# An audio tower with a shared and a routed feed-forward part on one core: the shared down product in three rounded products instead of one full-precision product

## The reference

```python
h = (ewma(x) + ewma_reversed(x)) * 0.5 @ W.T + b            # tokens: 16 x 750 rows of 256
h = h + selective_scan_two_layers(layernorm(h))             # 64 states
n = layernorm(h)
shared = (silu(n @ shared_gate_w.T) * (n @ shared_up_w.T)) @ shared_down_w.T   # 512 hidden
topk_idx, w = route(n)          # 16 experts in 4 groups, 2 groups and 4 experts of each token
routed = sum over the chosen experts e of w_e * (silu(n @ gate_w[e]) * (n @ up_w[e])) @ down_w[e]
out = h + shared + routed
```

## Time and profile before

| what | us |
|---|---|
| median of three runs (1314.46 to 1319.79) | 1316.31 |
| the profiled execution's own time | 1317.08 |
| its span, first to last instruction | 1314.9 |
| granted TensorE clock, mean | 0.943 of full speed |

### The profile page before, as it was taken

One profiled execution on the slowest core, in us unless ns is written; L12 is line 12 of the kernel. 1 busy time (PEld: TensorE's weight loads), 2 busy tenths in 40 slices (PEclk: granted clock), 3 DMA queues, 4 the chain that ended last, 5 costly groups with the idle time before them and its releaser, 6 DMA issues.

```text
span 1314.9 us, 24750 instructions
## 1 busy us (share of the span) xinstructions
PE 1167.5 (89%) x7477; PEld 1051.9 (80%) x7477; DVE 942.2 (72%) x2374; ACT 552.3 (42%) x899; POOL 415.4 (32%) x281
## 2 busy tenths in 40 slices
PE   3448877987999889998999899997999999989997
PEld 3337766866998789977988789977998899889997
DVE  6786898698668975888668975798578855644443
ACT  1524542552355333653355244553465343223332
POOL 2023162043212623153412623163302430343233
PEclk9658885998999989999999999999999999999999
DMA  4130021132021312231131323240221321243331
GB/s 124 32 88 24 17 69 36 44 84 56 12 55 33 99 50 53 42 83 45 31 70 31 79 54 53 42 98 26 42 62 34 91 38 38 55 104 56 53 50 20
DMA packets 88288, 71.48 MB, mean 54 GB/s; under 512 B 39671, under 2 KB 82848, under 8 KB 88168
## 3 DMA queue, kind: packets, MB, share of 16 engines
q1 hardware_dynamic: 58832, 43.30, 12.1%
q0 software_dynamic: 26832, 26.06, 11.9%
q10 hardware_dynamic: 2504, 0.55, 0.2%
HBM read 31.36 MB, written 39.34 MB: 54 GB/s over the span
## 4 chain that ended last, share of the span: by engine, by line
PE 66%; DVE 24%; issue 7%; ACT 1%; POOL 1%; DMA 0%; DVEq 0%; POOLq 0%; ACTq 0%
PE gu_ps L1692 18%; PE gu_ps L1665 14%; PE d_ps L1752 10%; PE d_ps L1733 8%; PE ch_ps L1642 3%; PE ch_ps L1720 3%; DVE h L1188 2%; DVE h L1196 2%; PE ch_ps L1573 2%; DVE stats L1202 1%; PE ch_ps L1712 1%; DVE h L1464 1%; DVE gu_ps L1453 1%; PE ch_ps L1603 1%; PE ch_ps L1591 1%
## 5 line engine op out<-in xcount | busy, mean ns | idle before, releaser
L804 POOL DMA_INDIRECT out_dram<-block_rows,entry x99 | 158.1, 1597 | 319.1 <-ACT block_rows L944 298.4
L1692 PE MATMUL gu_ps<-gu_hi,bx_hi 128*128 x792 | 238.7, 301 | 17.6 <-issue 17.6
L1692 PE MATMUL gu_ps<-gu_hi,bx_lo 128*128 x792 | 225.4, 285 | 0.0
L1692 PE MATMUL gu_ps<-gu_lo,bx_hi 128*128 x792 | 225.4, 285 | 0.0
L932 ACT ACTIVATE hid<-gu_ps 128x512 f32<-128x512 f32 (+1 forms) x195 | 115.1, 592 | 241.9 <-PE gu_ps L1692 108.7
L785 POOL DMA_INDIRECT lists<-records,pos x96 | 136.1, 1418 | 203.8 <-DVE pos L1361 177.9
L1733 PE MATMUL d_ps<-down,hid 128*125 128x256 f32 x768 | 185.3, 385 | 1.2 <-issue 1.2
L1692 PEld LDWEIGHTS gu_ps<-gu_hi,bx_hi 128*128 128x128 f32 x792 | 152.4, 192 | 26.1 <-issue 24.8
L1733 PEld LDWEIGHTS d_ps<-down,hid 128*125 128x125 f32 x768 | 140.7, 190 | 20.8 <-issue 1.8
L1692 PEld LDWEIGHTS gu_ps<-gu_hi,bx_lo 128*128 128x128 f32 x792 | 152.6, 193 | 1.2
L1692 PEld LDWEIGHTS gu_ps<-gu_lo,bx_hi 128*128 128x128 f32 x792 | 151.6, 191 | 0.0
(11 more groups left out here) (279 smaller groups left out, 2893.3 us busy)
## 6 DMA issues: line engine op xcount, KB each, us to landing
block_rows<-lists SPq DMA_DIRECT2D x99, 128.0 KB
out_dram<-h SPq DMA_DIRECT2D x24, 500.0 KB
t<-rstd_scratch SPq DMA_DIRECT2D x21, 250.0 KB, 5.2
x_in<-in_x_dram SPq DMA_DIRECT2D x8, 375.0 KB, 7.6
zt<-in_x_dram SPq DMA_DIRECT2D x7, 375.0 KB
entry<-lists SPq DMA_DIRECT2D x99, 8.0 KB, 2.5
out_dram<-block_rows,entry POOLq DMA_INDIRECT x99
lists<-records,pos POOLq DMA_INDIRECT x96
```

The lines of the kernel that those rows point to most:

```text
L804: pool.indirect_dma_start(out=out_rows[0:there, :], out_offset=bass.IndirectOffsetOnAxis(entry[n % UE][:, ID:ID + 1].bitcast(U32), 0), in_ ...
L1692: last = pe.matmul(gu_ps[:, 2 * (g % 2) + half, q * GH:(q + 1) * GH], a[n % 2][:, k, :], w[:, k, bass.ds(of, 1), half * GH:(half + 1) * GH ...
```

## The change

The down weights of the shared part are kept as a rounded part and a rest, both of type fp32r, and each fp32 matmul of `shared_down` becomes three fp32r matmuls. The parts of the hidden units are made by ScalarE (rounded, a copy) and GpSimd (rest, a subtraction), into the two buffers each that blocks use. `shared_down` waits for the rest (`s_lo`) instead of the hidden units. `hid`, the gathered rows and the finished blocks have rings of three instead of four. The group registers of up to two coming blocks are loaded behind a shared down product. Due ticks of some steps change, above all those of the list writes on GpSimd. `s_count(pair, n)` counts shared slots.

```diff
-    ("list", 0, dict(POOL=12.5)),
+    ("list", 0, dict(POOL=15.0)),
...
+    ("list", 1, dict(POOL=15.0)),
+    ("list", 2, dict(POOL=15.0)),
...
+    ("list", 3, dict(POOL=15.5)),
+    ("list", 4, dict(POOL=16.5)),
+    ("list", 5, dict(POOL=17.0)),
+    ("list", 7, dict(POOL=17.0)),
+    ("list", 6, dict(POOL=17.5)),
...
-    U, UE, UO = 4, 12, 4
+    U, UE, UO = 3, 12, 3
...
-        down = sb("down", [P, M, D])
+        down_hi, down_lo = (sb(f"down_{s}", [P, M, D], F32R) for s in ("hi", "lo"))
...
-        hid_t = sb("hid", [P, 4, 512])
+        NH = 3
+        hid_t = sb("hid", [P, NH, 512])
...
+            def shared_lo(pair, n, g):
+                wait(pool, "s_hi", s_count(pair, n))
+                inc(pool.tensor_tensor(hid_lo[g % 2][:, 0:TT], hid[g % NH][:, 0:TT],
+                                       hid_hi[g % 2][:, 0:TT].bitcast(F32), ALU.subtract), "s_lo")
+
             for k, before, g, amid in ticks("POOL"):
+                if g is not None and slot(g - 2)[0] == "S":
+                    shared_lo(*slot(g - 2)[1:], g - 2)
                 for event in before + amid:
...
-                was = slot(g - 4)
+                was = slot(g - NH)
                 if was[0] == "S":
-                    wait(act, "down_mm", done(g - 4))
+                    wait(act, "s_lo", s_count(*was[1:]))
...
+            def shared_hi(pair, n, g):
+                wait(act, "hid_done", done(g))
+                wait(act, "down_mm", done(g - 2))
+                inc(act.activation(hid_hi[g % 2][:, 0:TT], hid[g % NH][:, 0:TT], ACT.Copy), "s_hi")
...
                 run(amid)
                 if slot(g - 2)[0] == "B":
                     block_hi(slot(g - 2)[1], g - 2)
+                elif slot(g - 2)[0] == "S":
+                    shared_hi(*slot(g - 2)[1:], g - 2)
...
+            def groups_ahead(g):
+
+                ahead = []
+                for k in range(g + 1, g + 8):
+                    if slot(k)[0] == "S":
+                        break
+                    if slot(k)[0] == "B" and slot(k)[1] not in group_of:
+                        ahead.append(slot(k)[1])
+                for n in ahead[:2]:
+                    load_groups(n)
...
             def shared_down(pair, n, g):
                 m = n % M
-                wait(pe, "hid_done", done(g))
+                wait(pe, "s_lo", s_count(pair, n))
...
-                    last = pe.matmul(d_ps[0:TP, j, :], hid[g % 4][:, tc], down[:, m, :],
-                                     start=(m == 0 and j % 2 == 0), stop=(m == M - 1), skip_group_check=True)
+                    for c, (a, w) in enumerate(((hid_hi, down_hi), (hid_hi, down_lo), (hid_lo, down_hi))):
+                        last = pe.matmul(d_ps[0:TP, j, :], a[g % 2][:, tc], w[:, m, :],
+                                         start=(m == 0 and j % 2 == 0 and c == 0), stop=(m == M - 1 and c == 2),
+                                         skip_group_check=True)
                 inc(last, "down_mm")
...
                     shared_down(*slot(g - 3)[1:], g - 3)
+                    groups_ahead(g)
```

More of the change, by code:

```diff
@@ L133 @@
     (1, "table", 0): dict(DVE=14.5),
-    (0, "list", 0): dict(POOL=11.0),
+    (0, "list", 0): dict(POOL=15.0),
     (0, "ln1_stats", 0): dict(POOL=-26.5),
-    (0, "list", 8): dict(POOL=12.5),
+    (0, "list", 8): dict(POOL=15.0),
     (1, "ln2_norm", 1): dict(ACT=-1.5),
@@ L157 @@
     (0, "list", 11): dict(POOL=19.0),
[L158 to L161, removed]
+    (1, "list", 1): dict(POOL=15.0),
+    (1, "list", 2): dict(POOL=15.0),
+    (1, "list", 3): dict(POOL=15.0),
+    (1, "list", 4): dict(POOL=15.0),
     (1, "list", 5): dict(POOL=16.0),
@@ L174 @@
     (0, "spread", 0): dict(SP=-19.5),
-    (1, "list", 0): dict(POOL=11.5),
+    (1, "list", 0): dict(POOL=15.0),
     (1, "spread", 0): dict(SP=-26.0),
@@ L192 @@
     (1, "residual", 5): dict(DVE=-1.5),
+    (2, "list", 0): dict(POOL=15.5),
+    (0, "table", 0): dict(DVE=15.0),
+    (1, "entries", 0): dict(DVE=14.0),
+    (0, "list", 1): dict(POOL=16.0),
+    (0, "x2t", (0, 1)): dict(ACT=-3.0),
+    (0, "x2t", (1, 0)): dict(ACT=-0.5),
+    (0, "x2t", (1, 1)): dict(ACT=1.0),
+    (0, "ln2_norm", 2): dict(ACT=1.5),
+    (0, "x2t", (2, 0)): dict(ACT=3.0),
 }
@@ L216 @@
     (8.4, "routed", 4),
-    (11.4, "routed", 5),
+    (9.4, "routed", 5),
     (-6.7, "shared", 5),
@@ L365, in audio_tower_kernel @@
         states = sb("states", [P, 2, T], F32R)
-        hid_t = sb("hid", [P, 4, 512])
-        hid = [hid_t[:, n, :] for n in range(4)]
+        NH = 3
+        hid_t = sb("hid", [P, NH, 512])
+        hid = [hid_t[:, n, :] for n in range(NH)]
         hid_hi = [sb(f"hid_hi{n}", [P, 512], F32R) for n in range(2)]
@@ L583, in shared_part @@
                 return [w[:, n % KD, :].rearrange("p (m c) -> p m c", m=M) for w in pair_]
-            return down[:, :, (n % KD) * P:(n % KD + 1) * P], None
+            return [w[:, :, (n % KD) * P:(n % KD + 1) * P] for w in (down_hi, down_lo)]
         def shared_view(n):
@@ L931, in silu @@
                 hidden_is_free(g)
-                inc(act.activation(hid[g % 4][:, 0:n], gu_ps[:, 2 * (g % 2), 0:n], ACT.Silu), "silu_done")
+                inc(act.activation(hid[g % NH][:, 0:n], gu_ps[:, 2 * (g % 2), 0:n], ACT.Silu), "silu_done")
             def block_x(n, g):
@@ L1440, in shared_hidden @@
             def shared_hidden(g):
-                h = hid[g % 4][:, 0:TT]
+                h = hid[g % NH][:, 0:TT]
                 wait(dve, "prod_mm", done(g))
@@ L1454, in block_hidden @@
                 else:
-                    h = hid[g % 4].rearrange("p (e h) -> p e h", h=H)
+                    h = hid[g % NH].rearrange("p (e h) -> p e h", h=H)
                     wait(dve, "up_weighed", n + 1)
@@ L1698, in _, with load_groups @@
             group_of = {}
+            def load_groups(n):
+                if n in group_of:
+                    return
+                if n == first[iteration[n]]:
+                    wait(pe, "tabled", iteration[n])
+                group_of[n] = [pe.value_load(table[0:1, 3 * n + 1 + q:3 * n + 2 + q], min_val=0, max_val=NG - 1)
+                               for q in range(2)]
             def groups(g):
                 if slot(g)[0] == "B":
-                    n = slot(g)[1]
-                    if n == first[iteration[n]]:
-                        wait(pe, "tabled", iteration[n])
-                    group_of[n] = [pe.value_load(table[0:1, 3 * n + 1 + q:3 * n + 2 + q], min_val=0, max_val=NG - 1)
-                                   for q in range(2)]
+                    load_groups(slot(g)[1])
+            def groups_ahead(g):
[7 more added lines that the diff above has]
+                    load_groups(n)
             def block_x(n):
@@ L1719, in block_hidden @@
                 for m in range(4):
-                    last = pe.transpose(ch("bh", 0, n)[:, m * P:(m + 1) * P], hid[g % 4][:, m * P:(m + 1) * P], ident[:])
+                    last = pe.transpose(ch("bh", 0, n)[:, m * P:(m + 1) * P], hid[g % NH][:, m * P:(m + 1) * P], ident[:])
                 inc(last, "bh_mm")
```

39 lines of the change are left out of this document (16 added, 23 removed).

## The result

| | before | after |
|---|---|---|
| median, us | 1316.49 (1314.46 to 1319.79) | 1342.12 (1337.49 to 1345.98) |
| ratio, 95% interval | | 1.0196 (1.0165 to 1.0228) |
| span profiled, us | 1314.9 | 1344.2 |
| granted clock, mean | 0.943 | 0.929 |

The changed kernel is 2.0% slower. The forecast was 1306 us, with a range from 1283 to 1327; the time lies above both.

The account below looks back on a forecast made before the run. TensorE alone bounds ticks 0 to 11 and the tail, VectorE mostly ticks 12 to 20. 1317.1 - 15.3 (product) - 2 (registers) + 5 (VectorE) + 1.4 (prologue) = 1306 us, range 1283 to 1327.

Parts of the forecast that it names:

- so most are in time: GpSimd's rests: SiLU needs the buffer about 5 us after ScalarE's copy, so most rests would delay neither SiLU nor TensorE.
- the late train: Rival, chance 0.18: GpSimd's rests, list writes and smoothed-input addition end too late; 3 us a period, 18 us, 1324 us.
- The rival: The late train, chance 0.18: four rests stretched by 1 us each make 3 us a period, 1324 us in all.
- Rests of 1.2 us: GpSimd's 96 subtractions, 1.2 us each in proportion to a 750-column row of 1.80 us: 115 us of GpSimd's time.
- VectorE's port, +5 (0 to 29): VectorE loses 0.18 us per us of GpSimd subtractions, in its bound stretch only: 5 us lost, 0 to 29.
- The product, -15.3: Shared down product on TensorE, 1.73 us to 1.48: 0.25 us saved at 61 of 96 places on the chain, 15.3 us.
- Group registers, -2 (-12 to +24): Loads behind the shared down product: 12 us of gaps removed, 0.6 us sticking out at 17 places, net 2 us gained.
- ScalarE's copies, 0: 96 copies of 500 columns at 0.59 us, 57 us more on ScalarE, all hidden, costing nothing.
- Rings of three, 0: Rings of rows and finished blocks: nothing lost; 0 to 22 us if gathered rows landed late in the tail.
- Due ticks, 0: Moved due ticks of GpSimd's list writes, whose first waits 178 us for positions: no cost by itself.
- What would show it: Signs listed: ticks 0 to 11 shorter by some 2 us if right; TensorE or ScalarE's SiLU waiting for GpSimd if wrong.

Follow-up runs that it names:

- e1: The changed kernel without GpSimd's 96 rests, the third product taking the rounded part again: 1298.39 us, 0.9845 of the kernel before.
- e14: Kernel before with the changed due ticks, rings of three for rows and blocks, ScalarE's 96 copies unread, fp32 product, no loads ahead: 1311.73 us, 0.9957 of before.
- e13: e1 with the register loads put back between gate and up half: 1295.19 us, 0.9827 of the kernel before.
- e11: Kernel before with the changed due ticks, rings of three for rows and finished blocks, and registers loaded ahead, fp32 product: 1300.70 us, 0.9869 of before.
- e12: e11 with ScalarE's 96 rounded copies added, which nobody reads: 1294.61 us, 0.9863 of the kernel before.
- e5: The kernel before with only the due ticks of the changed kernel: 1307.88 us, 0.9946 of the kernel before.

## Why the prediction was wrong

**The sum.** In ratios, from kernel to kernel: due ticks -0.0054, rings +0.0012, loads -0.0089, copies -0.0006, product -0.0018, rests +0.0351; together +0.0196. The product's term includes the `hid` ring of three. Without the rests the time is 1298 us, where the forecast without its 5 us for VectorE would have been 1301. That this is near is luck: the product gave 2 us instead of 15 in this order, the loads ahead 9 to 12 instead of 2 and the due ticks 7 instead of nothing.

**The step that failed: the rests on GpSimd, "so most are in time", and the late train at 0.18.** The prediction had the mechanism, its place, its length (27.6 us to the end of the addition forecast, 27.4 measured), and its start: 582.1 in the times of before, where the changed kernel had slipped 17.7 us by then (SiLU of slot 15) and began at 599.77. What failed was the test for lateness. It held the train's end against the first token product on TensorE at 611.49. The due time is set earlier, by ScalarE's queue:
- The copy of the smoothed input stands ahead of the SiLU of slot 19. Before they started at 598.30 and 601.54. By the prediction's own sum the addition ends at 609.7 and the copy at 610.5, so that SiLU is 9 us late. Measured in pair 3, both delays together: the lag on e1 grows by 8.9 us from tick 15 to 19, and 2.3 come back later.
- The SiLU of slot 17, due at 590.27, waits for the rest of slot 14 behind four list writes and an output write. With the prediction's durations that is 582.1 + 1.2 + 4 x 1.72 + 1.9 + 1.2 = 593.3, so 3 us late. It had one sentence and no sum. Measured: 3.6 us in pair 3.

The rival priced this at 3 us a period and needed stretched rests for it. It needed none, as the train was no longer than forecast, and it cost 5.5 to 7.5 us a period in pairs 1 to 4. The prediction didn't look at pair 0 by itself: 14.4 us were lost up to tick 3 of pair 1, 8.1 of them before any list write. A train in fixed order has a due time for each member, not one for its end.

**Rests of 1.2 us.** The shape in proportion was nearly right for a rest alone (1.26 us at the median), but the mean is 1.42, as the group's row shows: 137 us, not 115. In 15 of the 96 the row starts before the output write ahead of it has ended; counted from that end they take 1.27 to 1.30 us, and the sum is 128 us. Nine others take 1.6 to 2.2 us (last section).

```profile
L821 POOL TENSOR_TENSOR hid_lo<-hid,hid_hi 128x500 fp32r<-128x500 f32 x96 | 136.7, 1424 | 336.7 <-ACT hid_hi L966 336.4
```

**VectorE's port, +5 (0 to 29).** Line 1188, on which the rate was read, did not change: its mean was 0.879 us and is 0.885 (line 1212 now). But VectorE as a whole is busy for 965.5 us, against 942.1 in e1 (page rows of both): 23 us for 137 us of rests, 0.17 us for each us. The prediction's 0.18 was the loss of line 1188 alone, so that the two rates agree is in part chance. How much of it is on the path no run tells apart.

```profile
L1212 DVE TENSOR_TENSOR h<-h,rows 125x512 f32<-125x512 f32 x48 | 42.5, 885 | 0.0
```

**The product, -15.3.** Right in isolation (16.5 us between e14 and e13; 1.40 to 1.51 us from its start to the next work in e13 over pairs 3 to 5, and 1.59 at tick 16, where 1.44 to 1.52 was forecast), wrong beside the loads. The prediction summed the two edits as if they were independent, and both need the time of the same product on TensorE.

**Group registers, -2 (-12 to +24).** Right in form. The gaps before line 1692 are mostly gone in e11 (17.6 us to 5.1 in its waits), the loads stick out by 0.5 us with fp32 in the mean of ticks 3 and 16 to 18, where 0.6 was taken, and yet the gain is 9 to 12 us. The SiLU times of e12 and e14 show where: from tick 17 to 22 e12 gains 2.4 to 3.1 us in each of pairs 2 to 5, where the gaps were counted at 1.9, and around ticks 17 and 18 it loses 0.6 to 1.5 us, where 1.2 was taken; 4.6 us more come in pair 1, which the count had left out. Behind three products no gain can be told (0.9845 against 0.9827, intervals overlap). In the changed kernel they still gain 8 us (1.0255 against 1.0196); that TensorE often waits for rests there anyway may be why, but no run shows it.

**ScalarE's copies, 0.** Right (e12). **Rings of three, 0.** Right with the new due ticks, wrong alone: 16 us by an output write, a wait that the prediction excluded because the list of waits before had none. **Due ticks, 0.** Wrong by 7 us gained. The prediction looked at the list writes' and not at the moved layer-norm power, before which GpSimd waits for 117 us in e5 instead of 182; which of the moved ticks gives the 7 us isn't shown.

**What would show it.** The prediction named ScalarE's SiLU waiting for GpSimd at ticks 17 to 19 as a sign of the train; that is what the timeline has. The stretch of the first slots is shorter by 1.3 us, where some 2 were expected.

## What to carry to other kernels

Before work is added to an engine with idle time, write out its queue in order across the place: an instruction that waits holds everything behind it, so idle time ahead of a waiting instruction can't be used, and the added work makes one train of what was spread. Then take for each member of the train its first reader, and what stands behind that reader on the reader's own queue; the earliest of these is the due time, and the member's end minus it is the loss in each period. Two edits that gain at the same instruction, one making it shorter and one hiding work behind it, are summed only after asking whether the shorter one still covers the other.

## What the runs showed of the hardware

- **Small VectorE operations can last as long as a GpSimd instruction beside them.** Line 1458 writes 11 integers from one input in SBUF and a constant; it takes 0.16 us, and the next time 2.20, from 609.15 to 611.35, where GpSimd's rest of line 821 ends at 611.32. It began while the output write ahead of the rest still ran (608.41 to 610.03); which of the two held it the rows don't tell. A sum of 125 x 4 values at line 1154, 0.16 us at the median, takes 2.66 us and ends at 627.22, where GpSimd's addition of 1.77 us ends at 627.19.

```profile
608.46 0.16 DVE L1458 TENSOR_SCALAR table<-route_t 1x11 int32<-1x11 f32 x1
...
609.15 2.20 DVE L1458 TENSOR_SCALAR table<-route_t 1x11 int32<-1x11 f32 x1
...
624.56 2.66 DVE L1154 TENSOR_TENSOR mv<-halves 125x4 f32<-125x4 f32 x1
```

  "SBUF — State Buffer" of the Trainium skill, section "Who interferes with whom", lists tensor_scalar among the operations that can take the port pair shared with GpSimd, when their operands meet its conditions; the trace agrees with 2.20 for 0.16 us. In these rows the length of the stall is that of GpSimd's instructions, not that of VectorE's.
- **GpSimd's rest is stretched beside a VectorE scan**: nine of the 96 rests begin 0.6 to 1.1 us after a scan of line 1194 over 750 steps with two inputs in SBUF, and take 1.6 to 2.2 us instead of 1.26.

```profile
567.00 1.71 DVE L1194 TENSOR_TENSOR_SCAN t<-zt,ut 128x750 f32<-128x750 f32 x1
567.60 2.17 POOL L821 TENSOR_TENSOR hid_lo<-hid,hid_hi 128x500 fp32r<-128x500 f32 x1 [4.97 <-ACT hid_hi L966]
```

- **Register loads cost more behind short matmuls**: at slot 13 of pairs 3 to 5, 0.9 us in the mean behind a product of eight fp32 rows and 1.4 behind one of twelve fp32r rows (0.7 and 1.6 in the pair shown). With loads behind it, the shorter product ended up 0.7 us longer in that pair. TensorE's queue seems to run less far ahead there; no run measured that by itself.
